# Padding rows of two sorted scratches written during attention instead of ahead of the first row of maxima, and the row places computed by GpSimd

## What is computed

```python
x = _layernorm(x + _L0_attn_ref(x, q_proj, k_proj, v_proj, o_proj))      # causal, 16 heads of 16
x = _layernorm(x + _L0_xattn_ref(x, itok, ctx, ctx, ctx))                # expert = token id range, 4 experts
x = _layernorm(x + _L0_ffn_ref(x, Wr, br, Wg, Wu, Wd))                   # top-1 router, 4 experts, 1024 wide
```

## Time and profile before

| what | value |
|---|---|
| three runs | 295.63 us median, 295.41 to 298.44 |
| the profiled execution: its own time | 298.62 us |
| its span (first to last instruction) | 296.7 us |
| outside the span | 1.9 us |
| mean granted PE clock | 0.917 of full |
| PE busy | 240.1 us (81% of the span) |
| DVE, ACT, POOL busy | 188.1, 135.3, 70.7 us |
| HBM read, written | 19.43 MB, 9.50 MB |

### The profile page before, as it was taken

One profiled execution on the slowest core, in us unless ns is written; L12 is line 12 of the kernel. 1 busy time (PEld: TensorE's weight loads), 2 busy tenths in 40 slices (PEclk: granted clock), 3 DMA queues, 4 the chain that ended last, 5 costly groups with the idle time before them and its releaser, 6 DMA issues.

```text
span 296.7 us, 7058 instructions
## 1 busy us (share of the span) xinstructions
PE 240.1 (81%) x2724; PEld 191.1 (64%) x2724; DVE 188.1 (63%) x421; ACT 135.3 (46%) x229; POOL 70.7 (24%) x132
## 2 busy tenths in 40 slices
PE   4995076988899897599997547998897999999970
PEld 3663064655666564368786422698686999999960
DVE  3888139587689675559988462689435555555550
ACT  3683033675594885356555150387021333333300
POOL 8730000100010354213122556000023122222222
PEclk9999669999999999869999557799799999999996
DMA  6799924252024445602409412340000000000000
GB/s 190 260 296 291 227 94 141 74 145 68 4 74 141 111 100 186 160 1 73 144 10 396 168 59 79 93 108 0 2 20 18 4 14 21 21 20 20 2 10 15
DMA packets 17424, 28.63 MB, mean 97 GB/s; under 512 B 2733, under 2 KB 12974, under 8 KB 17392
## 3 DMA queue, kind: packets, MB, share of 16 engines
q1 hardware_dynamic: 15952, 25.27, 29.1%
q0 software_dynamic: 1344, 2.90, 2.8%
q10 hardware_dynamic: 96, 0.00, 0.0%
HBM read 19.43 MB, written 9.50 MB: 98 GB/s over the span
## 4 chain that ended last, share of the span: by engine, by line
PE 58%; DVE 17%; issue 7%; DMA 7%; ACT 5%; POOL 3%; SPq 2%; POOLq 0%; DVEq 0%; ACTq 0%
PE ps L1300 9%; PE ps L1729 7%; PE ps L1730 7%; PE ps L1731 7%; PE ps L1746 4%; PE ps L1747 3%; PE ps L1748 3%; DMA arena<-arena 3%; PE ps L1401 2%; DVE arena L974 2%; DVE wf_lo L813 2%; PE ps L1665 2%; POOL sorted L532 2%; PE ps L1397 2%; ACT wf_hi L572 1%
## 5 line engine op out<-in xcount | busy, mean ns | idle before, releaser
L1730 PE MATMUL ps<-arena,wf_hi 128*128 128x128 f16 x352 | 60.2, 218 | 0.0
L1729 PE MATMUL ps<-arena,wf_hi 128*128 128x128 f16 x352 | 60.2, 219 | 0.0
L1731 PE MATMUL ps<-arena,wf_lo 128*128 128x128 f16 x352 | 60.2, 217 | 0.0
L1730 PEld LDWEIGHTS ps<-arena,wf_hi 128*128 x352 | 34.3, 98 | 0.2
L1729 PEld LDWEIGHTS ps<-arena,wf_hi 128*128 x352 | 33.7, 96 | 0.5 <-issue 0.4
L1731 PEld LDWEIGHTS ps<-arena,wf_lo 128*128 x352 | 33.9, 96 | 0.0
L1746 PE MATMUL ps<-wf_hi,arena 128*128 x88 | 24.8, 282 | 5.9 <-DVE arena L1237 3.4
L813 DVE SCALAR_TENSOR_TENSOR wf_lo<-ring,wf_hi 128x1024 f16<-128x1024 f32 x17 | 20.6, 1219 | 11.0 <-ACT wf_hi L572 5.9
L769 ACT ACTIVATE arena<-ps 128x512 f32<-128x512 f32 x22 | 13.1, 594 | 31.2 <-PE ps L1731 31.2
L1747 PE MATMUL ps<-wf_lo,arena 128*128 x88 | 24.8, 282 | 0.0
L1748 PE MATMUL ps<-wf_hi,arena 128*128 x88 | 24.7, 281 | 0.0
(11 more groups left out here) (230 smaller groups left out, 582.2 us busy)
## 6 DMA issues: line engine op xcount, KB each, us to landing
ring<-Wf SPq DMA_DIRECT2D x17, 512.0 KB, 3.7
sorted<-fill SPq DMA_DIRECT2D x1, 4515.0 KB, 24.2
arena<-Wf SPq DMA_DIRECT2D x7, 512.0 KB, 8.1
arena<-sorted SPq DMA_DIRECT2D x20, 129.0 KB, 2.2
sorted<-fill SPq DMA_DIRECT2D x1, 1161.0 KB, 7.0
ring<-xT SPq DMA_DIRECT2D x4, 256.0 KB, 5.5
X<-x_tok SPq DMA_DIRECT2D x1, 1024.0 KB, 8.0
ring<-ctxT SPq DMA_DIRECT2D x2, 512.0 KB, 3.8
```

Of the source, the lines that this page charges most:

```text
L1729: t.matmul(dst, hi, a_hi[p][:, k], start=k == 0, stop=False)
L1730: t.matmul(dst, hi, a_lo[p][:, k], start=False, stop=False)
L1731: last = t.matmul(dst, lo, a_hi[p][:, k], start=False, stop=k == NK - 1)
```

## The change

SP no longer fills both scratches ahead of `max_rows(0)`. It fills `sorted2` (one transfer, 9 tiles) in step 0, behind that step's loads, and `sorted3` in five transfers of 7 tiles, in steps 3, 4, 7, 8 and 11, each behind the loads of its step. The five count on a semaphore of their own. POOL's first scatter waits for the fill of `sorted2` alone, and a wait for the five stands ahead of the tiles of the second part in POOL's list. `pick` and the row places go from DVE (nine instructions) to POOL (eleven), behind its last low part of x. `pos_rdy` is now counted up by the two `places()` only, so the waits on it are one lower.

```diff
+FILL_AT, FILL_TILES = (3, 4, 7, 8, 11), 7
@@ SP
-            sp.wait_ge(fillrow, 1)
-            for scratch, rows in ((sorted2, NSA * P), (sorted3, NR3)):
-                sp.dma_start(scratch.rearrange("(n p) d -> p n d", p=P),
-                             fill[:, :].unsqueeze(1).to_broadcast([P, rows // P, ROW])).then_inc(filled, 16)
+            def pad(scratch, first, tiles_, done):
+                rows = scratch[first * P:(first + tiles_) * P, :].rearrange("(n p) d -> p n d", p=P)
+                sp.dma_start(rows, fill[:, :].unsqueeze(1).to_broadcast([P, tiles_, ROW])).then_inc(done, 16)
...
                 while n < min(used + RING, RING_CHUNKS):
                     load(n)
                     n += 1
+                if step == 0:
+                    sp.wait_ge(fillrow, 1)
+                    pad(sorted2, 0, NSA, filled)
+                elif step in FILL_AT:
+                    pad(sorted3, FILL_AT.index(step) * FILL_TILES, FILL_TILES, filled3)
@@ POOL, behind the last x_lo
+            pool.wait_ge(tile_rdy, 1)
+            link(g.tensor_tensor(pick[:, :, :], ge[:, 0:E, NA:NT], ge[:, 1:E + 1, NA:NT], ALU.subtract))
+            g.tensor_scalar(pick[:, :, :], pick[:, :, :], 1 / W_SCALE, None, ALU.mult).then_inc(pick_rdy, 1)
+            link(g.tensor_tensor(base_e[:, :], end_e[:, :], nt_e[:, :], ALU.subtract))
+            g.tensor_scalar(base_e[:, :], base_e[:, :], float(P), None, ALU.mult)
...
+            link(g.tensor_tensor(pos[:, 0:NA], where[:, 0:NA, 0], where[:, 0:NA, 1], ALU.add))
+            link(g.tensor_copy(pos_i[:, 0:NA], pos[:, 0:NA]))
...
-            pool.wait_ge(filled, 32)
-            pool.wait_ge(pos_rdy, 1)
+            pool.wait_ge(filled, 16)
...
+            pool.wait_ge(filled3, 16 * len(FILL_AT))
+
             def scatter3(part, i):
-                pool.wait_ge(pos_rdy, part + 2)
+                pool.wait_ge(pos_rdy, part + 1)
@@ DVE, behind maxima(1, 0)
-            link(v.tensor_tensor(pick[:, :, :], ge[:, 0:E, NA:NT], ge[:, 1:E + 1, NA:NT], ALU.subtract))
-            v.tensor_scalar(pick[:, :, :], pick[:, :, :], 1 / W_SCALE, None, ALU.mult).then_inc(pick_rdy, 1)
-            slots()
@@ PE
-            pe.wait_ge(pos_rdy, len(PARTS) + 1)
+            pe.wait_ge(pos_rdy, len(PARTS))
```

More of the change, by code:

```diff
@@ L61 @@
 WINDOW = 3
+FILL_AT, FILL_TILES = (3, 4, 7, 8, 11), 7
+assert len(FILL_AT) * FILL_TILES * P == NR3
 WARM_START, WARM_GAP = 24, 8
@@ L221, in build @@
             "const_z", "const_r", "const_s", "const_m", "const_q2", "row_z", "fillrow"))
-        filled = sem("filled")
+        filled, filled3 = sem("filled"), sem("filled3")
         w_hi, w_lo, x_hi, x_lo, c_hi, c_lo = (sem(n) for n in ("w_hi", "w_lo", "x_hi", "x_lo", "c_hi", "c_lo"))
@@ L491, in _ @@
                 g.tensor_tensor(xTv_lo[:, :, t], xT_st[:, :, t], xTv_hi[:, :, t], ALU.subtract).then_inc(x_lo, 1)
+            pool.wait_ge(tile_rdy, 1)
[3 more added lines that the diff above has]
+            g.tensor_scalar(base_e[:, :], base_e[:, :], float(P), None, ALU.mult)
+            link(g.tensor_tensor(run[:, :, 0:NA], run[:, :, 0:NA], cnt[:, :, 0:NA], ALU.subtract))
+            link(g.tensor_tensor(run[:, :, 0:NA], run[:, :, 0:NA], base_e[:, :].unsqueeze(2).to_broadcast([P, E, NA]),
+                                 ALU.add))
+            link(g.tensor_tensor(where[:, 0:NA, :], cum[:, 0:NA, :], run[:, :, 0:NA].rearrange("p e i -> p i e"),
+                                 ALU.add))
+            link(g.tensor_tensor(where[:, 0:NA, :], where[:, 0:NA, :], oh[:, 0:NA, :], ALU.mult))
+            link(g.tensor_tensor(where[:, 0:NA, 0:2], where[:, 0:NA, 0:2], where[:, 0:NA, 2:4], ALU.add))
+            link(g.tensor_tensor(pos[:, 0:NA], where[:, 0:NA, 0], where[:, 0:NA, 1], ALU.add))
+            link(g.tensor_copy(pos_i[:, 0:NA], pos[:, 0:NA]))
             def inv_std(var, n, out_sem):
@@ L838, in counts @@
                               ).then_inc(cnt_sb, 1)
[L840 to L850, removed]
             def logits(part):
```

## The result

| | before | after |
|---|---|---|
| first comparison, median (range) | 296.12 us (295.41 to 298.44) | 286.66 us (284.62 to 289.5) |
| second comparison | 294.72 us (292.36 to 296.91) | 284.48 us (282.25 to 286.75) |
| the profiled execution, its span | 298.62, 296.7 us | 284.87, 283.1 us |
| its mean granted PE clock | 0.917 | 0.954 |

The ratio is 0.9645 with a 95% interval of 0.9532 to 0.9758 in the first comparison, and 0.9636 (0.9578 to 0.9695) in the second, of more runs. So the change takes 9.5 to 10.2 us off. The forecast was 283.6 us by 12.0 us off; 286.66 lies in the range of 280.8 to 287.8, above the forecast's own of 281.8 to 285.4. The two profiles differ by 13.6 us of span, more than the medians do.

The account below looks back on a forecast made before the run. The prediction took PE's 11.04 us wait for batch 0's rows, queued behind padding, as the bound, with DVE behind it. 10.7 + 1.65 - 0.3 = 12.0 us off 295.63 gives 283.6 us; own range 281.8 to 285.4, wider 280.8 to 287.8.

Parts of the forecast that it names:

- What bounds the kernel: Step 0: all engines stand still for one transfer queue, PE waiting 11.04 us for batch 0's rows behind the padding.
- Rival 2: Step 0: batch 0's rows are slow by themselves, 7.9 us from issue; only 6.5 us gained, 289.1 us; chance 0.05.
- Part 1: Step 0: padding leaves the front of SP's list, rows land at 28.6 to 28.8; gain 10.7 us.
- Part 2: After the first reductions: nine small instructions leave DVE and come off in full; gain 1.65 us, bounds 1.0 and 1.65.
- Part 3: Eleven instructions on POOL behind line 491, 0.22 to 1.01 us each, hidden in its waiting; cost 0.
- the lock: POOL and DVE share ports exclusively, the loser blocked; if each of eleven held DVE 0.22 us, 2.4 us worse.
- Part 4: Six padding transfers in SP's list during the steps delay only batch 3's rows; cost 0.3 us, bounds 0 and 2.6.
- rival 1: Later rows inherit the queue: parts take 4.84 us, batch 3's rows come 2.0 to 2.6 us late; chance 0.17.
- The 3.7 us a part: Time assumed for one 7-tile padding transfer during the steps, between 3.4 and 3.9 us; slow end 4.84.
- 2t - 7.1: Step 12: lateness in us of batch 3's rows when each padding part takes t us.
- rival 3: Slower than before: padding beside chunks delays rows of three batches, eating all 12.3 us at t = 8.9; chance 0.03.
- The sum: Whole kernel: 10.7 + 1.65 - 0.3 = 12.0 us saved, taken from the 295.63 us median: 283.6 us.

Follow-up runs that it names:

- e1: The changed kernel with its second half undone: picks and row places back on DVE, new padding kept; 286.66 us in one execution.
- e4: The kernel before with all four rows of maxima of batch 0 issued by ACT, none by SP; 295.58 us in one execution.
- e9: The kernel before, unchanged, run once more for a second profile; 295.42 us, span 293.3.
- e5: The changed kernel, unchanged, timed and profiled once more; median 284.48 us.
- e10: The changed kernel with the 9 tiles of `sorted2` padding back ahead of the rows of batch 0; 284.69 us, ratio 0.9628.
- e6: The changed kernel with the fourth part of the `sorted3` padding in step 9 instead of step 8; median 284.44 us.

## Why the prediction was right, and where it missed

*What bounds the kernel*: right. With the padding out of the queue the rows of batch 0 land in 1.8 us (ACT's) and PE resumes at 28.67 (forecast 28.8). Rival 2, rows slow by themselves, is out: same rows, 7.9 and 1.8 us. (Under "what bounds the kernel" the wait was put down to one transfer queue. ACT's rows were in another queue and as slow, so a full queue of SP is not all of it.)

*Part 1*: right, even in what is late next. `stacks(3)` ends the next wait, `scores(1, 0)` starts at 30.22 (forecast 30.7), and the first reduction at 30.86 (31.4). The 0.5 us between are half explained by this execution being 0.24 us earlier ahead of the wait.

*Part 2*: 1.65 forecast, 1.64 measured, on the path in full. Together the two parts gave 12.9 us at `maxima(1, 1)` against 12.3 forecast. What the forecast did not have is the clock behind it: 1.4 to 1.6 us more in the executions where PE's wait for the nine was followed by a fall (`e1`, `e4`, `e9`), nothing against the profile it was read from.

*Part 3*: right. POOL's eleven cost 0.19 to 0.27 us each, about the low bound of 0.22, and DVE's reduction beside them (line 984 at 21.92) takes 1.23 us as before. The Trainium skill (SBUF — State Buffer, 🔬 SBUF: two separate sides) counts a DVE operation as a holder of the shared ports where it is in a two-port mode or has two SBUF inputs. The trace agrees: a reduction that reads PSUM neither slowed POOL nor was slowed. The forecast told the lock without this condition.

*Part 4*: the place was right (batch 3 alone, behind the parts of steps 7 and 8). The 0.3 us lies between what four executions showed (none in `e1` and `e5`, 0.16 in `e10`, 1.92 in the first), and rival 1's 2.0 to 2.6 us nearly came true once, without showing in the medians of `e5` and `e6`. The 3.7 us a part was somewhat low. The parts landed 6.7 to 10.5 us after their issue in the two profiles of the changed kernel, but with chunks in the same queue. `e10`'s 9 tiles took 5.8 us from issue to landing, which makes 4.5 us for 7 tiles, an estimate within the stated 4.84. By the forecast's own 2t - 7.1 the 1.92 us give t = 4.5 as well. In rival 3, 12.3 us are eaten at t = 8.6, not 8.9, where its delays are added up as in its 300 us at t = 10. That moves no chance. The windows put the DMA engines at full share from about 80 to 86 in the changed kernel's first profile, and from 82 to 88 in `e5`, with the rows issued at 83.46 and 86.03. How far the parts have drained by then seems to decide, which is argued and not shown.

*The sum* is where it missed, by 1.8 to 2.5 us. The step that failed is the sentence that the waits removed do not depend on the execution, "so the same saving gives 283.6". They do. In the old kernel the first matmul on the stacks comes 0.9 to 1.6 us behind the landing of the padding, at 35.91 to 38.96 in four executions, and whatever makes the front late is absorbed until then. The profile shown, at 298.62 us, was longer than any of the timed runs, and its padding took 24.2 us; others had 21.2 to 21.9. The new kernel has no such pin, and passes a front 2.6 us late on to `maxima(1, 1)` in full. So the gain at the first matmul on the stacks is 10.3 us between the first two profiles (38.96 and 28.67), but 5.7 between `e9` and `e5`, both with a late front (37.02 and 31.29). Of this difference of 4.6 us, 5.0 at `maxima(1, 1)`, most comes back in places that the forecast did not count on: `e9` and `e5` start the second part at 120.20 and 110.42, 9.8 us apart, where the first two profiles give 10.9 and the medians 10.2. It comes back by the clock that fell in `e9` behind the nine instructions (1.6 us), and by the stall in step 12 that `e5` did not have (1.9). Two errors of opposite sign are in the sum, then, and that it came as near as it did is partly luck.

The 3.0 us that the first profile lay above its median were put down to "no reason that the trace gives". Against `e9`, which lay at the median, the traces do give reasons: 0.9 us of a span 3.4 longer lies ahead of the second part, where the padding's 2.3 us and the clock behind the nine nearly cancel, and 2.5 us behind it, most of it the fall of the clock in the third part. That fall comes with and without the change (in two of the four profiles with the large padding ahead of the rows, in six of the other eight), so nothing makes it a part of the saving. How the timed runs divide between these causes stays open, as a timed run leaves no trace of its padding or its waits.

*The rest of the profiles' 13.6 us* is 12.9 from attention, less 1.9 in step 12, plus 2.6 from the first transpose of the second part on, of which 2.1 is the clock that held in this execution and fell in all the others that leave the place alone. The forecast named this stretch as one to watch.

Open stays what makes the padding's writes vary by 3 us and the first weights by 1.5 (the first projection starts between 6.63 and 8.18 us) between executions; no run changed that.

## What to carry to other kernels

A bulk transfer that nobody needs soon, issued ahead of a 2 KB one that an engine waits for, costs up to what is left of it at that moment (in this kernel 7 to 9 us for a 2 KB row, on either queue), and nothing if it has drained by then; move it only past those small transfers, and count how long each part drains in front of the next. A stall that is pinned to a transfer's end absorbs every delay ahead of it, so its length in one profile is no measure of what its removal brings: take the resume time from several executions, and expect the new kernel to pass on what the stall hid. Compare two profiles of the same kernel, stage by stage, before you add a gain from one of them to a median: here 2.5 of 3.4 us between two such profiles lay in stages that the change does not touch.

## What was not expected of the hardware

- The same 4515 KB of padding took 21.2, 21.7, 21.9 and 24.2 us to land in four executions, in the same place of the program.
- ACT's queue gave 2 KB copies no quick way past a full queue of SP: 7.2 to 7.9 us in the median of each profile, against 1.8 with the engines free. In the first profile they landed 3 to 5 us ahead of the padding, so they do not wait for its end, and are slow all the same. Issuing was slower as well, 1.4 us for the second and third in `e4`.
- PE's granted clock fell to 0.50 for some microseconds in the second part, after a gap of 1.4 to 1.8 us ahead of its first tile, in nine of the ten profiles without matmuls in that gap. It costs 1.0 to 2.1 us, and with eight unused matmuls in the gap it stayed at 1.00 in both profiles taken.
- Elsewhere it falls in some executions of a kernel and not in others: for 3.4 us behind PE's wait of 2 us in attention (three of four profiles, 1.4 to 1.6 us) and for 3.4 us in the third part (eight of twelve, 1.3 to 1.7 us).
